# Reordered loads, stores and norm steps, and one scale for a batch's context, in a fused gated cross-attention and mixture-of-experts kernel

## The chip, the cores and the metric

The kernel runs on one core of a Trainium2 chip. The metric is device time of one execution in microseconds (us). Five engines work side by side, each through its own list of instructions in order: PE (TensorE, matrix multiplications and transposes; PEld is its loading of weights), ACT (ScalarE), DVE (VectorE), POOL (GpSimd) and SP (SyncE, which here only issues DMAs). They hold each other up by semaphores alone: an instruction waits until a counter has reached a value, and everything behind it on its engine waits too.

## The reference

`x` has 16 batches of 224 rows of 512; `ctx` has 16 batches of 750 rows of 512; there are 8 experts of hidden size 256.

```python
x = x + jnp.tanh(g_xattn[0]) * _L0_xattn_ref(_layernorm(x), ctx_1024, ctx_1024)
#   h = einsum('eth,efh->etf', x, ctx);  a = gelu(h);  einsum('etf,efh->eth', a, ctx)
x = x + jnp.tanh(g_ffn[0]) * _L0_ffn_ref(_layernorm(x), gate_w, w1, w2, w3)
#   softmax(x @ gate_w), the two best experts of each row, silu(xs @ w1) * (xs @ w3) @ w2
```

The softmax weight of an expert multiplies the row before it enters the expert. All is float32. The kernel computes a float32 product from float16 pieces: each operand is scaled by a power of two and split into a high and a low half, and three of the four products of halves are added.

## The kernel before

**Two phases.** The first takes the batches one by one in a software pipeline of 16 steps (`batches`, all written out, and `last_step`); step i finishes the attention of batch i, prepares batch i + 1 and loads batch i + 2. The second takes 63 blocks of 128 routed rows through the experts (`step2`, `blocks`). The change touches the first phase only.

**A step of the first phase on PE** (line 1277): the scores of batch i in three thirds of the context (`scores`, L1210), the attention output in three thirds (`attend`, L1222), and between them the transposes of the next context (`trans_ctx`, L1177), of the second norm's rows of batch i − 1 (`rows_norm2`, L1196 from `xf`) and of the first norm's rows of batch i + 1 (`rows_norm1`, L1196 from `xn`), the router's logits of batch i − 2, and one-column sums over partitions (`ctx_total` L1184, `weight_total` L1191).

**The scale of the context.** For each third q of a batch's context, ACT forms the sum of squares of each partition (`ctx_squares`, L594), whose elementwise result goes to a part of `ctx_part` that is free at that time. POOL makes powers of two from the sums (`all_rows_scale`, L439 to L444, writing `ctx_s` and its inverse, three columns). ACT writes the high half, third by third (`ctx_high_part`, L624), and DVE the low half (`context_low`, L825), after which SP may load the next batch over it. PE adds the sums of all partitions, ACT copies the total (`ctx_tot_out`, L610), and POOL makes the scale of the attention from the largest of three totals (`context_scale`, L459 and on), which DVE needs in `context_factors` (L817 to L819).

**What else stands in a step.** The 24 expert matrices are squared, scaled and split on the way: `weight_squares` L603, `weight_scale` L935 to L940, `weight_high` L658, `weight_low` L949. A matrix is taken by `own_matrix` in each step; an odd step begins a second one (`split_begin`) and the following even step ends it (`split_end`), so that an even step has two `weight_scale` and two `weight_low`, and an odd step one of each. The norm of batch i + 1 is `stats1` (DVE, L802, L805), `inv_std` (POOL, L432, L434, writing `rstd`) and `norm1` (DVE, L848). POOL then sends the routes of batch i − 3 by four indirect DMAs (`send_routes`, L489), raises e to the logits' differences of batch i − 2 (`exps`, L473), and only then makes the context's scale for batch i + 2. `a_low` (L834) splits the attention weights, `residual` (L863) makes x2, `xnT_low` (L855) splits the transposed norm, `route_top` (L882 to L900) finds the two best experts.

**Order.** Every engine's order is written out by hand in its `step`. SP's `step` (line 342) issues: the store of x2, the load of x, the loads of two thirds of the context, the store of the norm, the load of the last third, then one or two expert matrices. Each of these waits for what it needs, in that order.

Of the kernel before, what the change touches and what calls it, by code (L numbers as in the profile page):

```python
# [93 lines left out]
def build(nc, x, ctx, g_xattn, g_ffn, gate_w, w1, w2, w3, out):  # L94
# [4 lines left out]
    with st:  # L99
# [36 lines left out]
        ctx_part = [[sb(f"ctx_part{u}{h}", [CR, NC, D], F16) for h in range(2)] for u in range(2)]  # L136
# [161 lines left out]
        def _(sp):  # L298
# [43 lines left out]
            def step(i, u, h, load_two=True):  # L342
                if later(i, 1):
                    store_rows(i - 1)
                    load_x(i + 1, 1 - u)
                if load_two:
                    for q in range(NQ - 1):
                        sp.wait_ge(ctx_split, i * NQ + (NQ + q + 1))
                        load_ctx(i + 2, q)
                if later(i, 1):  # L350
                    store_norm(i - 1)
                if load_two:
                    sp.wait_ge(ctx_split, i * NQ + 2 * NQ)
                    load_ctx(i + 2, NQ - 1)
                for n in ((3 * h + 3,) if u else (3 * h + 1, 3 * h + 2)):
                    if n >= 2:
                        load_weight(*matrix(n))
# [46 lines left out]
        def _(pool):  # L404
# [31 lines left out]
            def scale_from(gmax, inv, s, bits=0, n=1):  # L436

                exp, exp_i = exp_f[:, 0, 0:n], exp_f[:, 1, 0:n].bitcast(I32)
                seq.done(g.tensor_scalar(exp_i, gmax.bitcast(I32), 0.5 ** (MANT + 1), None, ALU.mult))  # L439
                seq.hold()  # L440
                seq.done(g.tensor_scalar(exp, exp_i, float(ROOT), float(1 << MANT), ALU.add, ALU.mult))
                seq.hold()
                seq.done(g.tensor_scalar(inv, exp, float((TOP - 1 + bits) << MANT), None, ALU.subtract))
                return g.tensor_scalar(s, exp, -1.0, float((2 * BIAS + TOP - 1 + bits) << MANT), ALU.mult, ALU.add)  # L444
# [6 lines left out]
            def all_rows_scale(i, u):  # L451

                hold(pool, ctx_sum_ready, i * NQ + NQ)
                scale_from(ctx_sum[:, :], ctx_inv[u][:, :], ctx_s[u][:, :], 0, NQ).then_inc(ctx_scaled, NQ)

            def context_scale(i):

                hold(pool, ctx_gsum_ready, i + 1)
                seq.done(g.tensor_scalar(ctx_max[:, :], ctx_gsum[:, 0:1], ctx_gsum[:, 1:2], ctx_gsum[:, 2:3], ALU.max, ALU.max))  # L459
                seq.hold()  # L460
                scale_from(ctx_max[:, :], all_inv[:, :], all_s[:, :], A_BITS).then_inc(all_scaled, 1)
# [119 lines left out]
        def _(act):  # L581
# [14 lines left out]

            def weight_squares(n, kind, e):
# [21 lines left out]
            def ctx_high_part(i, u, q):  # L619
# [4 lines left out]
                a.activation(ctx_part[u][0][:, c, :], ctx_raw[0:CR, c, :], ACT.Copy, scale=ctx_s[u][0:CR, q:q + 1].bitcast(F32)).then_inc(ctx_high, 1)  # L624

# [56 lines left out]
            def step(i, u, h):  # L682
# [16 lines left out]
                else:  # L699
                    ctx_high_part(i + 1, w, 0)  # L700
                    ctx_high_part(i + 1, w, 1)
# [3 lines left out]
                ctx_high_part(i + 1, w, 2)  # L705
# [16 lines left out]
                if two:  # L722
                    ctx_squares(i + 2, 0)
                    ctx_squares(i + 2, 1)
                ctxT_out(i + 1, w, 4)
                if two:
                    ctx_squares(i + 2, 2)
# [60 lines left out]
        def _(dve):  # L788
# [175 lines left out]
            def step(i, u, h):  # L964
# [13 lines left out]
                if later(i, 1):  # L978
                    a_low(i, u, 1)
                    norm2(j)  # L980
                    context_factors(i + 1, w)
                split_end(weight_scale, i, u, h)
                stats1(i + 1, w, (h + u) * 16 + 16)
                context_low(i + 1, w, 1)
                split_end(weight_low, i, u, h)
                context_low(i + 1, w, 2)
                own_matrix(weight_scale, i, u, h)
                a_low(i, u, 2)
                if not later(i, 1):
                    context_factors(i + 1, w)  # L990
                norm1(i + 1, w)
                if later(i, 2):
                    route_top(i - 2)
                own_matrix(weight_low, i, u, h)
                xnT_low(i + 1, i * 4 + 2, w, 0, H_ps[w])
                xnT_low(i + 1, i * 4 + 3, w, 1)
            batches(dve, step)
# [448 lines left out]
```

## Time and profile before

| | us |
|---|---|
| median of 3 timed runs | 682.88 (682.84 to 685.06) |
| profiled execution, its own time | 682.06 |
| its span in the trace | 680.4 |
| first phase, first scores of batch 1 to the scores of batch 15 | 45.49 to 348.37 |
| even step / odd step (from rank to rank on PE, 196.21, 218.54, 239.46) | 22.33 / 20.92 |
| PE, ACT, DVE, POOL busy over the span | 632.9, 459.6, 416.5, 396.6 |

The steps repeat almost to the hundredth of a microsecond, so one even and one odd step stand for all from step 3 on. Step 8 (even) runs from 196.30 to 218.62 on PE, step 7 (odd) lies before it and step 9 (odd) behind it. A start time to the next start time on an engine is what an instruction costs its engine; the duration in a row is longer, since neighbours overlap by a tenth of a microsecond. The figure in square brackets is the idle time of the engine before the row, and what ended it.

### The profile page before, as it was taken

To read this page: it belongs to the slowest core of one execution; us is meant where nothing else is said; L and a number is where in the kernel's file an instruction comes from. 1 tells how busy PE (TensorE), PEld (TensorE's weight loads), DVE (VectorE), ACT (ScalarE), POOL (GpSimd) and SP (SyncE) were. 2 spreads that over 40 slices of the span, in tenths; PEclk is the share of its full clock that TensorE was granted. 3 is DMA by queue.
4 is the path that set the end of the run, shared out by engine and by line. 5 is a ranking of instruction groups with operands and counts; after the bars stand their busy time and mean duration, and the time that the engine had idled before them with its cause. 6 is when DMAs were issued, how large, how long until landed. Compare 5 with 4: busy or idle time off the path is not lost.

```text
span 680.4 us, 15835 instructions
## 1 busy us (share of the span) xinstructions
PE 632.9 (93%) x4638; PEld 443.5 (65%) x4639; DVE 416.5 (61%) x1287; ACT 459.6 (68%) x771; POOL 396.6 (58%) x460
## 2 busy tenths in 40 slices
PE   2789999999999999999998999999999999999990
PEld 1677788788887888878875555555555545555540
DVE  3468788988889888898896644553333333333330
ACT  5899999899999999999974344444434434434440
POOL 4332347765676556665567587776546555665561
PEclk9999999999999999999999999999999999999996
DMA  7455558656776658656424576566666667666663
GB/s 213 134 173 154 157 159 192 185 155 154 193 173 170 185 129 222 168 159 186 127 90 106 106 126 110 105 108 120 121 121 108 118 117 123 108 113 119 110 115 53
DMA packets 51604, 95.04 MB, mean 140 GB/s; under 512 B 17184, under 2 KB 25504, under 8 KB 51536
## 3 DMA queue, kind: packets, MB, share of 16 engines
q1 hardware_dynamic: 34240, 60.02, 33.2%
q0 software_dynamic: 16480, 34.15, 28.1%
q8 instruction: 36, 0.59, 0.4%
q14 instruction: 32, 0.26, 0.2%
q10 hardware_dynamic: 816, 0.02, 0.1%
HBM read 62.15 MB, written 32.01 MB: 138 GB/s over the span
## 4 chain that ended last, share of the span: by engine, by line
PE 39%; DMA 5%; DVE 3%; issue 2%; ACT 1%; POOL 1%; DVEq 0%; SPq 0%; POOLq 0%; ACTq 0%
PE bank L1368 21%; PE bank L1377 11%; DMA out_rows<-ctx_raw,meta 4%; PE bank L1323 4%; PE bank L1357 2%; DMA ctx_raw<-xf_rows,meta 1%; DMA meta<-route_table 0%; PE bank L1257 0%; PE bank L1222 0%; DVE ctx_part L825 0%; POOL out_rows L537 0%; DVEq L1145 0%; ACT ctx_part L624 0%; ACT ctx_raw L766 0%; DVE x L863 0%
## 5 line engine op out<-in xcount | busy, mean ns | idle before, releaser
L1368 PE MATMUL bank<-w,ctxT 128*128 x756 | 173.5, 379 | 0.6 <-issue 0.6
L537 POOL DMA_INDIRECT out_rows<-ctx_raw,meta x63 | 100.3, 1592 | 94.0 <-DMA out_rows<-ctx_raw,meta 77.5
L1222 PE MATMUL bank<-ctx_part,a_part 125*112 125x512 f16 x576 | 135.1, 380 | 0.8 <-DVE a_part L834 0.8
L1368 PEld LDWEIGHTS bank<-w,ctxT 128*128 128x128 f16 x756 | 73.9, 98 | 75.7 <-issue 0.7
L1210 PE MATMUL bank<-xnT,ctxT 128*125 128x224 f16 x1152 | 117.7, 261 | 0.3 <-ACT ctxT L629 0.3
L1210 PEld LDWEIGHTS bank<-xnT,ctxT 128*125 128x125 f16 x1152 | 111.9, 138 | 0.4 <-issue 0.4
L777 ACT ACTIVATE ctxT<-bank,cols 128x256 f32<-128x256 f32 x63 | 29.9, 474 | 115.0 <-issue 90.0
L1222 PEld LDWEIGHTS bank<-ctx_part,a_part 125*112 125x112 f16 x576 | 71.4, 130 | 39.6 <-DVE a_part L834 0.8
L629 ACT ACTIVATE ctxT<-bank 128x1000 f16<-128x1000 f16 x96 | 94.5, 1006 | 2.5 <-PE bank L1177 2.5
L1377 PE MATMUL bank<-w2s,ctxT 128*128 x378 | 91.9, 379 | 1.4 <-DVE ctxT L1137 1.3
L489 POOL DMA_INDIRECT route_table<-route,pos_i x64 | 72.7, 1136 | 18.2 <-issue 18.2
L525 POOL DMA_INDIRECT ctx_raw<-xf_rows,meta x67 | 67.3, 1005 | 21.0 <-issue 17.7
L1146 DVE TENSOR_SCALAR cols<-Q,meta 128x2 f32 x63 | 15.0, 238 | 104.4 <-ACT ctx_raw L766 64.3
L766 ACT ACTIVATE ctx_raw<-bank,cols 128x512 f32<-128x512 f32 x63 | 43.4, 688 | 52.2 <-PE bank L1377 52.2
L1155 DVE SCALAR_TENSOR_TENSOR ctxT<-bank,cols,ctxT 128x256 f32<-128x256 f32 x63 | 30.5, 484 | 62.8 <-issue 49.5
L1377 PEld LDWEIGHTS bank<-w2s,ctxT 128*128 128x128 f16 x378 | 36.9, 98 | 46.5 <-issue 4.8
L825 DVE SCALAR_TENSOR_TENSOR ctx_part<-ctx_raw,ctx_s,ctx_part 125x1024 f16<-125x1024 f32 x48 | 60.3, 1272 | 8.3 <-ACT ctx_part L624 8.3
L834 DVE SCALAR_TENSOR_TENSOR a_part<-a_f,factors,a_part 125x448 f16<-125x448 f32 x48 | 32.8, 683 | 37.1 <-ACT a_part L643 37.0
L1177 PE MATMUL bank<-ident,ctx_part 125*128 125x125 f16 x768 | 53.6, 220 | 1.6 <-ACT ctxT L629 1.1
L624 ACT ACTIVATE ctx_part<-ctx_raw,ctx_s 125x1024 f16<-125x1024 f32 x48 | 53.1, 1135 | 1.9 <-POOL ctx_s L444 1.9
L1177 PEld LDWEIGHTS bank<-ident,ctx_part 125*128 125x128 f16 x768 | 48.1, 99 | 8.2 <-issue 1.3
L594 ACT ACTIVATE ctx_part<-ctx_raw 125x1024 f16<-125x1024 f32 x48 | 50.3, 1048 | 1.1
(155 smaller groups left out, 986.8 us busy)
## 6 DMA issues: line engine op xcount, KB each, us to landing
ctx_raw<-in_ctx SPq DMA_DIRECT2D x48, 448.0 KB
w_raw<-in_L_ffn_w SPq DMA_DIRECT2D x24, 512.0 KB, 6.3
x<-in_x SPq DMA_DIRECT2D x16, 448.0 KB, 6.5
out_rows<-x SPq DMA_DIRECT2D x16, 448.0 KB
xf_rows<-xf SPq DMA_DIRECT2D x16, 448.0 KB, 4.6
ctx_raw<-in_ctx SPq DMA_DIRECT2D x48, 52.0 KB
meta<-route_table SPq DMA_DIRECT2D x67, 1.0 KB, 2.5
ctx_raw<-xf_rows,meta POOLq DMA_INDIRECT x67, 4.2
```

The lines of the kernel that those rows point to most:

```text
L489: g.indirect_dma_start(out=table, out_offset=bass.IndirectOffsetOnAxis(ap=pos_i[v][:, m:m + 1], axis=0), in_=route[v][:, t, k, :], in_offs ...
L525: g.indirect_dma_start(out=xg[n % AHEAD], out_offset=None, in_=src, in_offset=bass.IndirectOffsetOnAxis(ap=meta[n][:, 0:1], axis=0)).then_ ...
L537: g.indirect_dma_start(out=out, out_offset=bass.IndirectOffsetOnAxis(ap=meta[n][:, 0:1], axis=0), in_=y_sb[n % 2], in_offset=None, compute ...
L594: a.activation(ctx_part[i % 2][1][:, 2 * q:2 * q + 2, :], ctx_raw[0:CR, 2 * q:2 * q + 2, :], ACT.Square, accum_out=ctx_sum[0:CR, q:q + 1]) ...
L624: a.activation(ctx_part[u][0][:, c, :], ctx_raw[0:CR, c, :], ACT.Copy, scale=ctx_s[u][0:CR, q:q + 1].bitcast(F32)).then_inc(ctx_high, 1)
L629: a.activation(ctxT[u][:, :, c * CS:c * CS + CR], T_half[c % 2], ACT.Copy).then_inc(ctxT_ready, 1)
L825: v.scalar_tensor_tensor(ctx_part[u][1][:, c, :], ctx_raw[0:CR, c, :], ctx_s[u][0:CR, q:q + 1].bitcast(F32), ctx_part[u][0][:, c, :], ALU. ...
L1177: ins = t_.transpose(T_half[c % 2][:, h * KD + k, :], ctx_part[u][h][:, c, k * P:(k + 1) * P], ident16[0:CR, 0:CR])
L1210: ins = t_.matmul(dst, ctxT[u][:, hc * KD + k, c * CS:c * CS + CR], xnT[u][:, hx, k, :], start=j == 0, stop=j == KD * len(PARTS) - 1)
L1222: ins = t_.matmul(O_ps[t][0:TT, :], a_part[ha][:, c, t * TT:(t + 1) * TT], ctx_part[u][hc][:, c, :], start=c == 0 and (ha, hc) == PARTS[0] ...
L1368: ins = t_.matmul(H_ps[u][:, :], rows, w, start=m == 0, stop=m == KD * len(PARTS) - 1)
L1377: ins = t_.matmul(O_ps[u][:, :], rows, w2s[:, bass.ds(e * (KH * 2 * D) + (2 * k + part[1]) * D, D)], start=m == 0, stop=m == KH * len(PART ...
```

## The change

- SP: the load of x goes ahead of the store of x2 (with the wait on `x2_ready` that `store_rows` had), and all three thirds of the context are loaded ahead of the store of the norm.
- ACT: from batch 2 on one activation of 3072 columns squares the whole context (`row_squares`), in place of three of 1024; its elementwise result goes to half of both buffers of `ctx_part`, now one tensor. The high half of the last two thirds is one activation of 2048 columns (`ctx_high_rest`), which stands ahead of the total and of the second gelu.
- POOL: one scale per partition, written to all three columns by a broadcast; one total in place of the largest of three.
- DVE: in each step `split_end(weight_scale)` moves ahead of `norm2`; `norm1` ahead of `a_low(2)`; `split_end(weight_low)` from between the two `context_low` to behind `a_low(2)`; `own_matrix(weight_low)` behind both `xnT_low`.

```diff
@@ SP step
                 if later(i, 1):
+                    sp.wait_ge(x2_ready, i * 2)
+                    load_x(i + 1, 1 - u)
                     store_rows(i - 1)
-                    load_x(i + 1, 1 - u)
                 if load_two:
-                    for q in range(NQ - 1):
+                    for q in range(NQ):
                         sp.wait_ge(ctx_split, i * NQ + (NQ + q + 1))
                         load_ctx(i + 2, q)
                 if later(i, 1):
                     store_norm(i - 1)
-                if load_two:
-                    sp.wait_ge(ctx_split, i * NQ + 2 * NQ)
-                    load_ctx(i + 2, NQ - 1)
@@ POOL
-                scale_from(ctx_sum[:, :], ctx_inv[u][:, :], ctx_s[u][:, :], 0, NQ).then_inc(ctx_scaled, NQ)
+                scale_from(ctx_sum[:, 0:1], ctx_inv[u][:, :], ctx_s[u][:, :], 0, 1, NQ).then_inc(ctx_scaled, NQ)
...
+                gmax = ctx_gsum[:, 0:1]
+                if not later(i, 2):
+                    gmax = ctx_max[:, :]
+                    seq.done(g.tensor_scalar(gmax, ctx_gsum[:, 0:1], ctx_gsum[:, 1:2], ctx_gsum[:, 2:3], ALU.max, ALU.max))
@@ ACT
+            def row_squares(i, u):
+                for q in range(NQ):
+                    act.wait_ge(ctx_loaded[q], i * 32 + 32)
...
+                a.activation(ctx_both[u][:, :, 0:NC // 2, :], ctx_raw[0:CR, :, :].rearrange("p (h c) d -> p h c d", h=2), ACT.Square,
+                             accum_out=ctx_sum[0:CR, 0:1]).then_inc(ctx_sum_ready, NQ)
+            def ctx_high_rest(i, u):
+                act.wait_ge(ctx_scaled, i * NQ + NQ)
+                a.activation(ctx_part[u][0][:, 2:NC, :], ctx_raw[0:CR, 2:NC, :], ACT.Copy, scale=ctx_s[u][0:CR, 0:1].bitcast(F32)).then_inc(ctx_high, NQ - 1)
...
                     ctx_high_part(i + 1, w, 0)
-                    ctx_high_part(i + 1, w, 1)
+                    ctx_high_rest(i + 1, w)
                     ctx_tot_out(i + 1)
                     gelu(i, u, 1)
                 split_end(weight_tot_out, i, u, h)
-                ctx_high_part(i + 1, w, 2)
...
                 if two:
-                    ctx_squares(i + 2, 0)
-                    ctx_squares(i + 2, 1)
+                    row_squares(i + 2, u)
                 ctxT_out(i + 1, w, 4)
-                if two:
-                    ctx_squares(i + 2, 2)
                 ctxT_out(i + 1, w, 5)
@@ DVE step
                     a_low(i, u, 1)
+                split_end(weight_scale, i, u, h)
+                if later(i, 1):
                     norm2(j)
                     context_factors(i + 1, w)
-                split_end(weight_scale, i, u, h)
                 stats1(i + 1, w, (h + u) * 16 + 16)
                 context_low(i + 1, w, 1)
-                split_end(weight_low, i, u, h)
                 context_low(i + 1, w, 2)
                 own_matrix(weight_scale, i, u, h)
-                a_low(i, u, 2)
...
                 norm1(i + 1, w)
+                a_low(i, u, 2)
+                split_end(weight_low, i, u, h)
                 if later(i, 2):
                     route_top(i - 2)
-                own_matrix(weight_low, i, u, h)
                 xnT_low(i + 1, i * 4 + 2, w, 0, H_ps[w])
                 xnT_low(i + 1, i * 4 + 3, w, 1)
+                own_matrix(weight_low, i, u, h)
```

On DVE, in the middle of an even step, from the statistics of the next batch's rows (`stats`, `mv`) to the norm itself (`xn`), before:

```order
L802 BN_STATS stats<-x 112x6 x2
L805 BN_AGGR mv<-stats 112x2 x2
L825 SCALAR_TENSOR_TENSOR ctx_part<-ctx_raw,ctx_s,ctx_part 125x1024
L945 COPY w_inv<-w_scales 128x1
L949 SCALAR_TENSOR_TENSOR w<-w_raw,w_scales,w 128x4x256
L825 SCALAR_TENSOR_TENSOR ctx_part<-ctx_raw,ctx_s,ctx_part 125x1024
L935 TENSOR_SCALAR w_exp<-w_gsum 128x1
L937 TENSOR_SCALAR w_exp<-w_exp 128x1
L939 TENSOR_SCALAR w_scales<-w_exp 128x1
L940 TENSOR_SCALAR w_scales<-w_exp 128x1
L834 SCALAR_TENSOR_TENSOR a_part<-a_f,factors,a_part 125x448
L848 TENSOR_SCALAR xn<-x,mv,rstd 112x512 x2
```

The same place of the changed kernel, whose line numbers are higher by some 18 (L866 is the norm, L852 `a_low`, L967 `weight_low`):

```order
L820 BN_STATS stats<-x 112x6 x2
L823 BN_AGGR mv<-stats 112x2 x2
L843 SCALAR_TENSOR_TENSOR ctx_part<-ctx_raw,ctx_s,ctx_part 125x1024 x2
L953 TENSOR_SCALAR w_exp<-w_gsum 128x1
L955 TENSOR_SCALAR w_exp<-w_exp 128x1
L957 TENSOR_SCALAR w_scales<-w_exp 128x1
L958 TENSOR_SCALAR w_scales<-w_exp 128x1
L866 TENSOR_SCALAR xn<-x,mv,rstd 112x512 x2
L852 SCALAR_TENSOR_TENSOR a_part<-a_f,factors,a_part 125x448
L963 COPY w_inv<-w_scales 128x1
L967 SCALAR_TENSOR_TENSOR w<-w_raw,w_scales,w 128x4x256
```

A `weight_low` and an `a_low` that stood ahead of the norm stand behind it.

On DVE again, at the end of an even step, from the last instruction of `route_top` (`R`) to `residual` (`x`), before:

```order
L900 TENSOR_TENSOR R<-R,M 112x8
L945 COPY w_inv<-w_scales 128x1
L949 SCALAR_TENSOR_TENSOR w2s<-w_raw,w_scales,w2s 128x2x512
L855 SCALAR_TENSOR_TENSOR xnT<-bank,xnT 128x4x112 x2
L863 SCALAR_TENSOR_TENSOR x<-bank,factors,x 112x512 x2
```

The same place of the changed kernel:

```order
L918 TENSOR_TENSOR R<-R,M 112x8
L873 SCALAR_TENSOR_TENSOR xnT<-bank,xnT 128x4x112 x2
L963 COPY w_inv<-w_scales 128x1
L967 SCALAR_TENSOR_TENSOR w2s<-w_raw,w_scales,w2s 128x2x512
L881 SCALAR_TENSOR_TENSOR x<-bank,factors,x 112x512 x2
```

The step's own `weight_low` has changed places with the two `xnT_low`.

On ACT, from the squares at the end of an odd step (`ctx_sum` is the sum) to the middle of the next, even one, before:

```order
L594 ACTIVATE ctx_part,ctx_sum<-ctx_raw 125x1024 x2
L629 ACTIVATE ctxT<-bank 128x8x125
L594 ACTIVATE ctx_part,ctx_sum<-ctx_raw 125x1024
L629 ACTIVATE ctxT<-bank 128x8x125
L639 ACTIVATE a_f<-bank,factors 125x448
L643 ACTIVATE a_part<-a_f,factors 125x448
L624 ACTIVATE ctx_part<-ctx_raw,ctx_s 125x1024 x2
L610 ACTIVATE ctx_gsum<-bank 128x3
L639 ACTIVATE a_f<-bank,factors 125x448
L643 ACTIVATE a_part<-a_f,factors 125x448
L617 ACTIVATE w_gsum<-bank 128x1
L624 ACTIVATE ctx_part<-ctx_raw,ctx_s 125x1024
```

The same place of the changed kernel:

```order
L609 ACTIVATE ctx_part,ctx_sum<-ctx_raw 125x2x1536
L649 ACTIVATE ctxT<-bank 128x8x125 x2
L659 ACTIVATE a_f<-bank,factors 125x448
L663 ACTIVATE a_part<-a_f,factors 125x448
L639 ACTIVATE ctx_part<-ctx_raw,ctx_s 125x1024
L644 ACTIVATE ctx_part<-ctx_raw,ctx_s 125x2048
L625 ACTIVATE ctx_gsum<-bank 128x3
L659 ACTIVATE a_f<-bank,factors 125x448
L663 ACTIVATE a_part<-a_f,factors 125x448
L632 ACTIVATE w_gsum<-bank 128x1
```

The squares are one instruction, and 1024 more columns of the context's high half stand between the first gelu (the first `a_f`, `a_part`) and the second.

## Rows read from the trace of the kernel before

**Rows 1.** The page, busy time of each engine over the span:

```profile
PE 632.9 (93%) x4638; PEld 443.5 (65%) x4639; DVE 416.5 (61%) x1287; ACT 459.6 (68%) x771; POOL 396.6 (58%) x460
```

**Rows 2.** Windows of step 8 and step 9: length, then busy time per engine:

```profile
196.30:218.62 22.32, 21.46 (x200) 17.95 (x198) 19.11 (x61) 20.60 (x33) 13.99 (x19) 1.00 0.68 180
218.62:239.55 20.93, 20.93 (x199) 17.79 (x196) 18.04 (x57) 20.51 (x33) 13.64 (x19) 1.00 0.61 168
```

**Rows 3.** Timeline of PE and its weight loads, steps 0 and 8 (start, duration):

```profile
40.75 0.60 PE L1196 MATMUL bank<-ident,xn 112*128 112x112 f32 x4 [1.23 <-DVE xn L848]
...
211.89 0.39 PEld L1196 LDWEIGHTS bank<-ident,xf 112*128 112x128 f32 x4 [0.35 <-issue]
...
213.80 0.60 PE L1196 MATMUL bank<-ident,xn 112*128 112x112 f32 x4 [0.86 <-DVE xn L848]
```

**Rows 4.** Timeline of ACT, steps 7 and 8:

```profile
182.87 0.67 ACT L643 ACTIVATE a_part<-a_f,factors 125x448 f16<-125x448 f32 x1
183.44 1.13 ACT L624 ACTIVATE ctx_part<-ctx_raw,ctx_s 125x1024 f16<-125x1024 f32 x1
...
201.00 2.17 ACT L624 ACTIVATE ctx_part<-ctx_raw,ctx_s 125x1024 f16<-125x1024 f32 x2
...
217.00 1.05 ACT L594 ACTIVATE ctx_part<-ctx_raw 125x1024 f16<-125x1024 f32 x1
...
223.33 2.17 ACT L624 ACTIVATE ctx_part<-ctx_raw,ctx_s 125x1024 f16<-125x1024 f32 x2
```

**Rows 5.** Timeline of DVE, steps 7, 8 and 14:

```profile
183.57 0.69 DVE L834 SCALAR_TENSOR_TENSOR a_part<-a_f,factors,a_part 125x448 f16<-125x448 f32 x1 [0.27 <-ACT a_part L643]
...
187.07 2.45 DVE L825 SCALAR_TENSOR_TENSOR ctx_part<-ctx_raw,ctx_s,ctx_part 125x1024 f16<-125x1024 f32 x2
...
204.49 0.69 DVE L834 SCALAR_TENSOR_TENSOR a_part<-a_f,factors,a_part 125x448 f16<-125x448 f32 x1 [0.27 <-ACT a_part L643]
...
208.49 1.25 DVE L825 SCALAR_TENSOR_TENSOR ctx_part<-ctx_raw,ctx_s,ctx_part 125x1024 f16<-125x1024 f32 x1
...
209.72 1.27 DVE L949 SCALAR_TENSOR_TENSOR w<-w_raw,w_scales,w 128x1024 f16<-128x1024 f32 x1
...
213.20 1.00 DVE L848 TENSOR_SCALAR xn<-x,mv,rstd 112x512 f32<-112x512 f32 x2
...
215.92 1.27 DVE L949 SCALAR_TENSOR_TENSOR w2s<-w_raw,w_scales,w2s 128x1024 f16<-128x1024 f32 x1
217.11 1.14 DVE L855 SCALAR_TENSOR_TENSOR xnT<-bank,xnT 128x448 f16<-128x448 f32 x2
...
334.23 0.69 DVE L834 SCALAR_TENSOR_TENSOR a_part<-a_f,factors,a_part 125x448 f16<-125x448 f32 x1 [0.27 <-ACT a_part L643]
...
347.98 1.40 DVE L863 SCALAR_TENSOR_TENSOR x<-bank,factors,x 112x512 f32<-112x512 f32 x2
```

**Rows 6.** Timeline of POOL, steps 7 and 8:

```profile
195.45 2.96 POOL L473 TENSOR_TENSOR ex<-euler,dl 112x16 f32<-112x16 f32 x1
199.14 0.26 POOL L439 TENSOR_SCALAR exp_f<-ctx_sum 128x3 int32<-128x3 int32 x1 [0.73 <-ACT ctx_part L594]
...
209.98 1.61 POOL L434 TENSOR_TENSOR rstd<-ve,neg_half 112x2 f32<-112x2 f32 x1
...
216.11 1.89 POOL L489 DMA_INDIRECT route_table<-route,pos_i  x1 [0.30 <-issue]
218.02 2.97 POOL L473 TENSOR_TENSOR ex<-euler,dl 112x16 f32<-112x16 f32 x1
221.46 0.26 POOL L439 TENSOR_SCALAR exp_f<-ctx_sum 128x3 int32<-128x3 int32 x1 [0.48 <-ACT ctx_part L594]
...
222.55 0.19 POOL L444 TENSOR_SCALAR ctx_s<-exp_f 128x3 int32<-128x3 f32 x1
...
223.19 0.73 POOL L434 TENSOR_TENSOR rstd<-ve,neg_half 112x2 f32<-112x2 f32 x1
```

**Rows 7.** Transfers into the raw context (the second phase's gathers among them), issue to landing:

```profile
DMA to landing us min/median/max: 3.3/4.8/6.2
```

## What was predicted

> **What bounds the kernel now.** I read the page first: PE is busy for 93% of the span, no other engine for more than 68% [rows 1]. The second phase isn't touched, so the question is what limits a step of the first. The windows of one even and one odd step answer half of it: in the odd step PE is busy for all of its 20.93 us, in the even step for 21.46 of 22.32 [rows 2]. The timeline of PE shows the hole in the even step: 0.86 of waiting for `xn`, DVE's norm, and just before it 0.35 in its weight loads [rows 3]. Without both an even step would take PE 21.1, an even and an odd step (a pair) 42.05 in place of 43.25.
>
> Who else needs most of a pair? ACT is busy for 20.5 us of each step [rows 2], but what matters is a ring that passes through ACT, DVE and POOL once per step. I follow it from where ACT begins the high half of the context (201.00) to where it does so a step later (223.33) [rows 4]. Two thirds and the second gelu: DVE starts `a_low(1)` at 204.49, so 3.49. DVE's chain to the end of the statistics, where `context_low(1)` starts: 208.49, so 4.00. POOL's `inv_std` and four route DMAs up to `exps` at 218.02: 9.53. `exps` 2.97. Then POOL waits 0.48 for ACT's squares, of which I count 0.1 as the hold itself, and makes the scale from 221.46 to 222.74: 1.28. ACT takes it up 0.59 later, 0.05 more than none [rows 4 to 6]. Without the two spare pieces (0.38 and 0.54) the ring needs 21.4 of the even step's 22.33. In the odd step, the same way: 3.49 again, then 183.57 to 187.07 is 3.50, to 195.45 is 8.38, 2.96, 0.1, 1.28, 0.05: 19.75 of 20.92, spare 1.17. So the ring of a pair needs 41.2: the slack under PE's own 42.05 is 0.9 us, and this kernel has a second limit right below the first.
>
> **The change part by part.**
>
> *Norm sooner.* In the even step DVE ends the second `context_low` 1.26 sooner, since a `weight_low` (209.72, 1.27 long) leaves, and the `a_low` of 0.6 ahead of the norm leaves too. The norm at 213.20 could start 1.8 sooner; but it needs POOL's `rstd`, which ends at 211.59 (209.98 + 1.61) [rows 5, 6], and there it stays: the gain is 1.6 against 0.86 + 0.35 of waiting, so PE's hole goes. What is late next is `a_low(2)`, which now follows the norm: the third `attend` needs it some 1.65 after the norm starts, when PE is 0.8 beyond its first `xn` transposes; that is a tie within 0.1.
>
> *One activation of 3072 for the squares.* ACT's 1.05 for 1024 columns [rows 4] and its slope, (1.13 − 0.67) over 576 columns, 0.80 ns each [rows 4], make 2.7 for the whole against three times 1.05: 0.45 less. It is hidden in both kinds of step, where ACT then waits for PE or for POOL. Bounds of the long one: 2.5 to 3.1.
>
> *One activation of 2048 for the rest of the high half.* It costs ACT 1.0 + 0.82 in place of 1.0 + 1.0, and no one waits for the last third earlier than it comes now. But 1024 columns of it now stand ahead of the second gelu, on the ring. That is +0.82 (0.80 to 1.04 by the rows used) on 3.49, in every step. The ring becomes 22.25 + 20.55 = 42.8: above PE's 42.05. So the second limit takes over.
>
> *One total, one scale.* One POOL instruction fewer before `context_factors`; DVE gets there later than POOL anyhow: nothing. The squares end sooner, so POOL's waits of 0.48 and 0.73 for them go; they were the spare pieces counted above.
>
> *Loads ahead of stores.* x comes some 0.4 sooner, the last third of the context without the norm's 448 KB ahead. Neither is waited for in the trace of before, so nothing gained; the stores behind them are wanted a step later. The matrices are loaded later, since `weight_low` moves to the step's end; the load that waits for it on SP stands ahead of the next load of x, but that one waits for `residual`, which is behind `weight_low` on DVE: nothing more is held. The matrix is squared in the next step only, behind both its first gelus: nothing, or some tenths.
>
> *`weight_low` behind `xnT_low`.* This is what I think costs. POOL's instructions are held when they start inside a long DVE one: `rstd`'s power takes 1.61 when it starts in `weight_low` and 0.73 when nothing runs, and the route DMA at 216.11 takes 1.89, ending as the `weight_low` of 215.92 has ended [rows 5, 6]. In the changed even step, counted from the norm's start n: norm and `route_top` 2.72 (213.20 to 215.92), `a_low(2)` 0.6, `weight_low` 1.25, two `xnT_low` 1.07; so the last `weight_low` runs from n + 5.6 to n + 6.85. POOL: a first route DMA to n + 1.5 (held by the norm as now), a second that now starts in the first `weight_low` and ends at n + 3.65, then two free ones of 0.95 with gaps of 0.3: `exps` starts at n + 6.2, in the middle of `weight_low`, and is held for 0.65. The route DMAs lose less than now (about 0.2 less), and `rstd` 0.05. In the odd step, where the first `weight_low` is missing and `xnT_low` waits for ACT, the same durations put `weight_low` at n + 4.85 to n + 6.05 and `exps` at n + 5.3: held 0.7. So even 22.25 + 0.65 − 0.25 = 22.65, odd 20.55 + 0.7 = 21.25: a pair takes 43.9, 0.65 more than before. Of this hold no row shows `exps` itself: it takes 2.96 or 2.97 in both steps [rows 6]. The bounds are no hold (42.55 a pair, −0.7) and a hold of `exps` and then of the scale's last instruction by the next `a_low(0)`, 0.4 a step (44.65, +1.4). I take 43.9, since the nearest row, a POOL power that starts in a `weight_low`, was held to its end.
>
> The Trainium skill, SBUF — State Buffer, section "Who interferes with whom", says that a VectorE instruction with two SBUF inputs contends with a GpSimd instruction that reads SBUF, and one with at most one SBUF input does not. The held rows agree. By that page `exps` would be held (43.9 a pair); by its own rows, which show 2.97 at most, 42.55.
>
> *The ends.* Step 0: PE waits 1.23 for `xn` [rows 3]; the norm now goes ahead of `a_low(2)`, and 1.1 comes back. Steps 1 and 2 have no routes for POOL to send, so their ring is short: step 1 gets ACT's savings, some 0.3, step 2 its hole of 1.2 less 0.2 for the tie. Together −2.4 (−1 to −3). After step 14, DVE's residual opens the block map from which the second phase's loads are made. It is 13.75 behind `a_low(1)` now (334.23 to 347.98), with no idle time between [rows 5]; the same instructions remain, `a_low(1)` is 0.85 later in the ring and the norm waits 0.2 for `rstd`: +1.05.
>
> **The sum.** Five pairs (steps 4 to 13): 5 × 0.65 = +3.25; −2.4 + 3.25 + 1.05 = +1.9. The profiled execution took 682.06, which makes 684.0; the median of the runs before is 682.88, 0.8 above it, so I forecast 684.8. With the bounds of a pair alone: −4.85 to +5.65, so 678 to 688.5.
>
> **The rivals.**
>
> *PE stays the only limit.* POOL's second route DMA starts only 0.2 us behind the beginning of `weight_low`; if it gets in ahead of it, the chain behind it is 0.75 shorter, `exps` comes before the last `weight_low`, and the ring is 42.05 or less. For it: margins of 0.2 are what I can't place; the odd step's POOL chain has room today. Against: the long activation on the ring is certain. The time: 5 × −1.2, −2.4 and at the end +0.6: −7.8, 675.1.
>
> *The ring binds, but `exps` is not held*, as its own rows have it: −0.7 a pair, 678.
>
> *Slower: ACT waits for the context.* The one squaring needs all three thirds; before, the last third was wanted 3 us later than the first. The squares begin 3.8 behind the norm now (213.20 to 217.00) and would begin 4.0 behind it [rows 4, 5]; the last third is issued some 0.7 ahead of the norm, so it has 4.7 to land. The median of the tile's transfers is 4.8 and the longest 6.2 [rows 7]. At the longest ACT is 1.5 late in each step, and from there it is ACT's path, not POOL's, that sets the ring: 22.2 + 22.7 = 44.9 a pair, 5 × 1.65 − 2.4 + 1.05 = +6.9, 689.8. It decides as soon as a landing takes over 4.7 + 0.6. Against: one 448 KB store fewer ahead of it.
>
> **How the numbers follow.** The forecast's mechanism gets 0.52 (its own range 681 to 688.5), PE alone 0.22, the ring without the hold 0.12, the late context 0.10; 0.04 is left for what I don't see. A measurement of this kernel tells about 0.5%, 3.4 us, from no change: below 679.5 is faster, above 686.3 slower. Faster: PE alone 0.22, of the third 0.07: 0.29. Slower: 0.09 of the late context and 0.16 of the forecast, whose upper end has `a_low(0)` holding the scale: 0.25. The same: 0.46. The range reaches from 675, which leaves half of the PE case out, to 689.5.
>
> **What would show it.** POOL's first scale instruction behind `exps` has no wait for ACT any more; ACT's first third waits for POOL's `ctx_s` in each step; `exps` takes 3.5 or more where it took 2.97; PE waits for `xn` in the odd steps too, some 0.5 to 1; a pair from rank to rank is near 43.9. I am wrong if PE has no waits (PE alone), if `exps` is 2.97 everywhere, or if ACT's squaring waits for a DMA.

## The result and the profile after

Six runs of the changed kernel took 691.76 us in the median (690.44 to 692.23), six of the kernel before beside them 682.86 (681.14 to 687.06). The ratio is 1.0118, 95% interval 1.0096 to 1.014: slower by 1.2%, and 2 us beyond the range that was given. The profiled execution took 691.75 us, its span is 690.0 us.

The page's busy line answers to [rows 1]: ACT and POOL do less than before (450.7 for 459.6, 381.0 for 396.6), PE more (641.5 for 632.9) with the same count of PE's instructions.

```profile
PE 641.5 (93%) x4638; PEld 446.1 (65%) x4639; DVE 418.4 (61%) x1287; ACT 450.7 (65%) x701; POOL 381.0 (55%) x446
```

The windows of steps 8 and 9, from rank to rank, answer to [rows 2] (length, busy time of PE, PEld, DVE, ACT and POOL, granted clock, share of the DMA engines, GB/s). The even step lost 0.25, the odd one 0.93, and PE is now short of its window in both (0.82 and 0.35 idle). The loss is in part longer busy time: of the odd step's 0.93 the idle time is 0.35.

```profile
198.62:221.19 22.57, 21.75 (x199) 18.00 (x197) 18.72 (x59) 20.12 (x28) 13.21 (x18) 1.00 0.68 167
221.19:243.05 21.86, 21.51 (x197) 17.85 (x195) 18.77 (x58) 20.16 (x28) 12.52 (x18) 1.00 0.76 171
```

By PE's rank products the whole account is short. At the start of step 3 the changed kernel is 0.79 us ahead, at the start of step 15 it is 5.74 behind (354.02 against 348.28), at the first product of the second phase 8.59 (377.15 against 368.56), at the end of the span 9.6. So the twelve steps 3 to 14 lose 6.5 us (pair 44.37 in place of 43.28), and step 15 and what follows 3.

ACT's waits, summed over the run (us, times, longest), hold two lines that before did not exist:

```profile
ACT ctx_part L609 <- DMA ctx_raw<-in_ctx: 10.9, 10, 1.9
ACT ctx_part L609 <- PE bank L1241: 2.1, 3, 0.7
```

The second is the same wait: there, too, ACT starts 0.22 to 0.23 behind the landing of the last third (by the semaphore records of the trace), and the `attend` that is named had been done before. So ACT waited for the load ahead of 13 of its 14 squarings of a whole context, 13.1 us in all. One turn shows where this sits. ACT's timeline of step 8 (answers to [rows 4]; L609 is the one squaring, L644 the 2048 columns, L659 a gelu):

```profile
204.10 1.13 ACT L639 ACTIVATE ctx_part<-ctx_raw,ctx_s 125x1024 f16<-125x1024 f32 x1
205.15 1.99 ACT L644 ACTIVATE ctx_part<-ctx_raw,ctx_s 125x2048 f16<-125x2048 f32 x1
...
207.09 0.62 ACT L659 ACTIVATE a_f<-bank,factors 125x448 f32<-125x448 f32 x1
...
220.74 2.76 ACT L609 ACTIVATE ctx_part<-ctx_raw 125x3072 f16<-125x3072 f32 x1 [0.96 <-DMA ctx_raw<-in_ctx]
```

DVE's in the same step (answers to [rows 5]): the second `a_low`, the last two low parts, the norm, and at the end the own matrix's `weight_low` ahead of the residual.

```profile
208.44 0.68 DVE L852 SCALAR_TENSOR_TENSOR a_part<-a_f,factors,a_part 125x448 f16<-125x448 f32 x1 [1.14 <-ACT a_part L663]
...
212.50 2.45 DVE L843 SCALAR_TENSOR_TENSOR ctx_part<-ctx_raw,ctx_s,ctx_part 125x1024 f16<-125x1024 f32 x2
...
215.63 1.01 DVE L866 TENSOR_SCALAR xn<-x,mv,rstd 112x512 f32<-112x512 f32 x2 [0.18 <-issue]
...
221.28 1.28 DVE L967 SCALAR_TENSOR_TENSOR w2s<-w_raw,w_scales,w2s 128x1024 f16<-128x1024 f32 x1
222.48 1.40 DVE L881 SCALAR_TENSOR_TENSOR x<-bank,factors,x 112x512 f32<-112x512 f32 x2
```

SP's queue issues the last third 0.03 after DVE has let its room go, and the norm's store 0.80 behind it:

```profile
214.98 0.76 SPq L308 DMA_DIRECT2D ctx_raw<-in_ctx  x2
...
215.78 0.34 SPq L340 DMA_DIRECT2D xf_rows<-xf  x1
```

The low parts end at 214.95. The third lands at 220.52 by its semaphore record, 5.54 behind its issue, and ACT, which was ready at 219.78, starts at 220.74. That is a ring: first third of the high part (204.10) to `a_low` 4.34, to the end of the low parts 6.51, from there through the load to ACT's start 5.79, squaring to the next first third (226.52) 5.78, together 22.42, where PE alone would need 21.1. In the steps in which ACT waited, the way from the end of the low parts to ACT's start took 5.4 to 6.7 us, of which the third's own time from issue to landing was 5.2 to 6.5 (median 5.5).

[rows 7] has no such load in it. Before, as after, the profile lists the loads of the context without a landing time (the first line, of the kernel before); the 4.8 is made of the second phase's gathers into the same tile and of writes of output rows that read it:

```profile
ctx_raw<-in_ctx SPq DMA_DIRECT2D x48, 448.0 KB
ctx_raw<-xf_rows,meta POOLq DMA_INDIRECT x67, 4.2
out_rows<-ctx_raw,meta POOLq DMA_INDIRECT x63, 4.9
```

By the semaphore records of the trace before, the last third took 5.4 to 6.5 us from issue to landing in steps 3 to 14 as well. In step 8 it was issued at 212.22, landed at 217.58, and its squaring began at 220.17, so there were 2.4 us to spare; over these steps 1.6 to 2.4.

POOL's `exps` (answers to [rows 6]) are held in the odd steps and free in the even ones, and the first scale instruction still waits for ACT in the even ones:

```profile
198.01 3.97 POOL L477 TENSOR_TENSOR ex<-euler,dl 112x16 f32<-112x16 f32 x1
...
220.57 2.97 POOL L477 TENSOR_TENSOR ex<-euler,dl 112x16 f32<-112x16 f32 x1
...
223.76 0.25 POOL L438 TENSOR_SCALAR exp_f<-ctx_sum 128x1 int32<-128x1 int32 x1 [0.23 <-ACT ctx_part L609]
```

PE still waits for the norm, 0.33 to 0.71 in nearly every step, the odd ones too (answers to [rows 3]); the last row is step 15's:

```profile
216.24 0.60 PE L1215 MATMUL bank<-ident,xn 112*128 112x112 f32 x4 [0.71 <-DVE xn L866]
...
238.10 0.60 PE L1215 MATMUL bank<-ident,xn 112*128 112x112 f32 x4 [0.35 <-DVE xn L866]
...
362.02 4.16 PE L1241 MATMUL bank<-ctx_part,a_part 125*112 125x512 f16 x12 [1.25 <-DVE a_part L852]
```

### The profile page after: what moved, and what is told of

It is laid out like the page before. It is cut to its first block, busy times and chain, and to the rows that moved or that the text cites. A ratio compares the mean times of both kernels' runs of the same rounds, so it can differ in the third digit from the quotient of the medians.

```text
span 690.0 us, 15723 instructions
## 1 busy us (share of the span) xinstructions
PE 641.5 (93%) x4638; PEld 446.1 (65%) x4639; DVE 418.4 (61%) x1287; ACT 450.7 (65%) x701; POOL 381.0 (55%) x446
## 4 chain that ended last, share of the span: by engine, by line
PE 38%; ACT 15%; DVE 14%; DMA 13%; issue 12%; POOL 6%; DVEq 1%; SPq 0%; ACTq 0%; POOLq 0%
PE bank L1387 19%; PE bank L1396 10%; DMA ctx_raw<-in_ctx 7%; DMA out_rows<-ctx_raw,meta 5%; ACT ctx_part L644 4%; DVE ctx_part L843 3%; PE bank L1342 3%; ACT ctxT L649 3%; DVE stats L820 2%; ACT a_f L659 2%; PE bank L1241 2%; DVE xf L895 2%; PE bank L1376 2%; ACT ctx_part L639 2%; ACT a_part L663 1%
## 5 line engine op out<-in xcount | busy, mean ns | idle before, releaser
L1241 PE MATMUL bank<-ctx_part,a_part 125*112 125x512 f16 x576 | 137.1, 384 | 2.0 <-DVE a_part L852 1.9
L1241 PEld LDWEIGHTS bank<-ctx_part,a_part 125*112 125x112 f16 x576 | 71.7, 130 | 44.1 <-DVE a_part L852 4.8
L649 ACT ACTIVATE ctxT<-bank 128x1000 f16<-128x1000 f16 x96 | 92.8, 1003 | 3.1 <-PE bank L1196 3.1
L493 POOL DMA_INDIRECT route_table<-route,pos_i x64 | 62.2, 972 | 19.8 <-issue 14.2
L431 POOL TENSOR_SCALAR ve<-mv 112x2 f32<-112x2 f32 x32 | 19.9, 623 | 70.2 <-DVE mv L823 69.5
L852 DVE SCALAR_TENSOR_TENSOR a_part<-a_f,factors,a_part 125x448 f16<-125x448 f32 x48 | 32.7, 681 | 38.3 <-ACT a_part L663 36.1
L477 POOL TENSOR_TENSOR ex<-euler,dl 112x16 f32<-112x16 f32 x14 | 47.3, 3378 | 4.7 <-DVE dl L909 4.5
```

The costliest lines, as they stand in the source:

```text
L477: ins = g.tensor_tensor(ex[:, :, :].rearrange("p t e -> p (t e)"), euler[:, :], dl[:, :, :].rearrange("p t e -> p (t e)"), ALU.pow)
L493: g.indirect_dma_start(out=table, out_offset=bass.IndirectOffsetOnAxis(ap=pos_i[v][:, m:m + 1], axis=0), in_=route[v][:, t, k, :], in_offs ...
L649: a.activation(ctxT[u][:, :, c * CS:c * CS + CR], T_half[c % 2], ACT.Copy).then_inc(ctxT_ready, 1)
L1241: ins = t_.matmul(O_ps[t][0:TT, :], a_part[ha][:, c, t * TT:(t + 1) * TT], ctx_part[u][hc][:, c, :], start=c == 0 and (ha, hc) == PARTS[0] ...
```

## The experiments

Theory A: the ring just shown, closed by ACT's one squaring that waits for the last third. Theory B: the forecast's ring over POOL with `exps` held. C: SP's order of transfers. D: the place of the own `weight_low` in DVE's order. Each kernel was timed in five rounds; ratios are to the kernel before, with their 95% intervals.

**Parts alone (e1, e2, e3) and the squaring's wait taken away (e4b).**

e1, the DVE part of the change alone:

```
+ split_end(weight_scale, i, u, h)    # ahead of norm2
  norm1(i + 1, w)
+ a_low(i, u, 2)
+ split_end(weight_low, i, u, h)
  ...
  xnT_low(i + 1, i * 4 + 3, w, 1)
+ own_matrix(weight_low, i, u, h)
```

> The kernel before with VectorE's new order alone (norm1 ahead of the third a_low and of the split matrix's weight_low, the own matrix's weight_low last); squares, scales and SyncE's order as before. Theory A (the loss of the changed kernel is ScalarE's one squaring waiting for the context's last third, so the loop runs through that load): the last squaring here needs only 0.95 us behind its third, so the loop has no such ring; the steps take 43.2 to 43.4 us a pair as before, the end gains or loses up to 3 us (the residual of batch 14 stands behind one more weight_low): 682 to 686. Theory B (the forecast's ring over POOL, with the exponentials held by the moved weight_low): the exponentials take 3.9 us instead of 2.96 in odd steps, and the pair grows by 0.65: 685 to 688.

686.39 us, 1.0051 [1.0035, 1.0066]. The profiled execution has a pair of 44.1, but unevenly: steps of 21.1 and steps of 23 to 24.6. In the long ones ACT waits up to 1.27 us for the last third (4.0 in all), or PE up to 1.79 us for the norm. The longest of them shows why, in DVE's timeline: the statistics wait for x, which SP issued at 221.78 behind a matrix (220.07) and a store.

```profile
232.38 1.29 DVE L802 BATCH_NORM_STATS2 stats<-x 112x6 f32<-112x512 f32 x2 [2.57 <-DMA x<-in_x]
```

So DVE's order alone costs, in the steps too, which A had not expected. The time lies inside B's range (685 to 688) and just outside A's, but not by B's mechanism: `exps` are held (3.97 or 3.98) in only three of the twelve steps, and ACT waits for POOL's scale `ctx_s` twice in the whole run. The granted clock also falls to 0.50 twice (at 205 to 207 and at 239 to 241), which is a part of the loss. The place of the own `weight_low` (D) fits the wait for x just shown; e1 moves other instructions too, so it doesn't show D by itself.

e2, SP's part alone:

```
+ sp.wait_ge(x2_ready, i * 2); load_x(i + 1, 1 - u)
  store_rows(i - 1)
+ for q in range(NQ): ... load_ctx(i + 2, q)    # all three
  store_norm(i - 1)
```

> The kernel before with SyncE's new order alone (x ahead of the store of the rows, the context's last third ahead of the store of the norm). Theory A: the last third is issued 0.1 to 1 us earlier and shares the DMA engines with the norm's store, its landing stays 4.8 to 5.8 us; ScalarE's last part of squares (0.95 us) has room: 682 to 684, pair 43.2. Theory B: no part of POOL's ring changes: 682 to 684. A theory C, that the order of the transfers itself costs the time: 686 or more here.

682.62 us, 0.9997 [0.9985, 1.0008], pair 43.28: nothing. C falls.

e3, ACT's and POOL's part alone, the orders of DVE and SP as before:

```
- def step(i, u, h):  # VectorE, SyncE: new order
+ def step(i, u, h):  # VectorE, SyncE: order of before
```

> The changed kernel with VectorE's and SyncE's order of before, so only one squaring, one scale, and thirds 1 and 2 of the high parts in one instruction. Theory A: the squaring still waits for the last third (issued after the norm's store): ScalarE waits for DMA ahead of it in most steps, pair 44 or more, 687 to 692. Theory B: exponentials are not held (2.96 in odd steps too), POOL does fewer scales, the pair falls to 42.8: 679 to 683.

707.0 us, 1.0373 [1.0351, 1.0396], pair 46.1: nearly three times the change's loss. ACT waits 10.9 us for the last third, and PE again 0.86 for the norm in most steps. B, which wanted a gain, falls here. The size is beyond A's 692. Part of the rest is in ACT's waits for DVE's `weight_scale`, 24.9 us in the run for 13.2 before: in DVE's order of before it stands behind `norm2`, and the 2048 columns delay the gelu ahead of that (argued from the orders, not tested by itself). In most even steps they take 1.57 and 1.02; ACT's copy `xfT` stands behind them, and PE waits 1.3 to 1.8 for it in six (11.3 us in the run for `xfT`). One step of 27.57 ran partly at a lower granted clock (0.88 over the step).

e4b, the change with a squaring that reads the first third three times:

```
- for q in range(NQ): act.wait_ge(ctx_loaded[q], i * 32 + 32)
+ act.wait_ge(ctx_loaded[0], i * 32 + 32)
- ctx_raw[0:CR, :, :].rearrange(...)
+ ctx_raw[0:CR, 0:1, :].rearrange(...).to_broadcast([CR, 2, NC // 2, D])
```

> The changed kernel, whose squaring reads the first third three times over instead of the three thirds once, so it has the same size and place but waits for the first third alone; the waits for the other two stand ahead of the high parts in the next step. The scale is that of a third of the context here. Theory A: ScalarE no longer waits for DMA ahead of the squaring, the pair falls by about 1.1 from 44.4 to 43.3 or below; what is left against before is the end (about +3): 683 to 686. Theory B: the ring over POOL stands unchanged, exponentials 3.97 in odd steps: 690 to 692.

682.56 us, 1.0003 [0.9985, 1.0021]: the 8.9 us by which the change was behind the kernel before are gone with that wait alone, a little more than A had (683 to 686). B's 690 to 692 falls. (`exps` take 2.96 in most of its steps, with DVE's order unchanged, so that order alone doesn't fix the hold.) Its squarings never wait and still take 2770 ns. Undisturbed pairs take 42.36; two of the six take 44, where ACT waited 0.99 and 0.55 for a matrix that came late. The windows of one good and one bad pair (length, PE):

```profile
173.19:194.22 21.03, 21.03 (x198) 17.86 (x196) 18.57 (x58) 20.06 (x28) 13.52 (x18) 1.00 0.71 177
194.22:215.55 21.33, 21.33 (x200) 18.05 (x197) 18.71 (x59) 19.83 (x28) 12.42 (x18) 1.00 0.73 172
215.55:237.39 21.84, 21.45 (x198) 17.94 (x195) 18.64 (x58) 19.80 (x28) 13.28 (x18) 1.00 0.76 175
237.39:259.65 22.26, 21.56 (x200) 18.02 (x197) 18.72 (x59) 19.96 (x28) 13.60 (x18) 1.00 0.64 165
```

**The ring shortened (e5), the own `weight_low` moved back (e6, e7), and three squarings (e8).**

```
e5  - ctx_high_rest(i + 1, w)            # 2048 columns ahead of the gelu
    + ctx_high_part(i + 1, w, 1)
      ctx_tot_out(i + 1); gelu(i, u, 1); split_end(weight_tot_out, i, u, h)
    + ctx_high_part(i + 1, w, 2)
e6  + own_matrix(weight_low, i, u, h)    # ahead of the two xnT_low again
      xnT_low(...); xnT_low(...)
    - own_matrix(weight_low, i, u, h)
e7  both;   e8  before, with SP's new order and DVE's as in e6
```

> The changed kernel with thirds 1 and 2 of the high parts in two instructions again, third 2 behind the split matrix's total as before; one squaring and one scale stay. Theory A with the ring squaring, scale, high parts, second gelu, a_low, VectorE's last two low parts, load of the last third, next squaring: this ring is shorter by 0.85 us a step (the second gelu no longer stands behind 2048 columns), the waits for DMA ahead of the squaring (10.9 us in ten) mostly go, pair 43.0 to 43.5, 683 to 687. Theory D (what costs is only where VectorE splits the own matrix, not the ring): 690 to 692.

> The changed kernel with the own matrix's weight_low ahead of the two xnT_low again. Theory A: the ring over the last third stays as it is and so do most of the waits for it, pair 44.0 to 44.4; the end gains about 2 to 3 us, since the residual of batch 14 and the first map come sooner: 687 to 690. Theory D (SyncE's next weight load and x stand behind that weight_low in its queue, and that delays the rest): x lands sooner, the exponentials take 2.96 in odd steps, TensorE no longer waits for xn, pair 43.0 to 43.4: 682 to 685.

> Both edits at once: own weight_low ahead of xnT_low, and the high parts of thirds 1 and 2 in two instructions. Theory A: the ring has a slack of half a us, pair 42.4 to 43.0, the end as before: 676 to 681. Theory D: what e6 gives, and no more: 682 to 685.

> The kernel before (three squarings, three scales, high parts in three) with SyncE's new order and VectorE's norm1 ahead of the third a_low and of the split matrix's weight_low, but the own matrix's weight_low left ahead of xnT_low. Theory A: only the last third's own squaring (1.05 us) follows its load, no wait for it; xn comes 2 us sooner and the 0.7 to 1.3 us a pair that TensorE waited for it go: pair 42.1 to 42.6, 675 to 680. Theory D: the same, since the own weight_low is where it was. Theory B (ring over POOL with its three scales): 43.3, 682 to 684.

e5: 679.23 us, 0.995 [0.9931, 0.997], pair 42.56; e6: 689.46, 1.0105 [1.0081, 1.0128], pair 44.55; e7: 679.81, 0.9964 [0.9948, 0.998], pair 42.98; e8: 681.51, 0.9987 [0.9978, 0.9997], pair 43.34. Against the kernel before, timed beside each, the change is 8.9 us behind and e5 2.8 ahead: 0.85 us of ACT's work, taken off the ring and put behind the gelu, gives back 11.7 us, near the 14 × 0.85 = 11.9 of a ring that sets every step. That is more than A had for e5 (683 to 687), and D's 690 to 692 falls. ACT still waits for the third, 10.2 us ahead of 13 squarings (6.1 of it under that name in the profile), but what is left of these waits is mostly no longer PE's. The 0.85 are taken off the ring over POOL as well, so e5 alone doesn't tell A from B; e4b does, and ACT's waits for `ctx_s`, two of 1.8 us together in the changed kernel, both in the first steps. With the own `weight_low` ahead of `xnT_low` PE gets the last half of the norm late, up to 1.2 us in every second step, as e8 shows at the start of its scores:

```profile
219.56 0.69 PE L1209 MATMUL bank<-xnT,ctxT 128*125 128x224 f16 x5 [1.08 <-DVE xnT L853]
```

So the ring of A stands, and D is wrong about the steps: its 682 to 685 for e6 falls, and norm sooner pays only with that `weight_low` last (e8 against the pair of e12 below). A's ranges hold for e6 and e7 (e6's pair is a little longer than the 44.0 to 44.4 expected). For e8 A's 675 to 680 was too low: PE waits 7.7 us there for `xnT`, in seven places. e8's time and pair are those that B gave, but ACT waits for `ctx_s` only twice there, so its mechanism is not seen.

**The end (e10), the norm's store (e11), and the orders without the one squaring (e12, e13).**

```
e10  e5, and  + if i == B - 2: own_matrix(weight_low, i, u, h)   # step 14, ahead of xnT_low
              - own_matrix(weight_low, ...)                      # last, in the other steps
e11  e10, and SP:  load_weight(...)
                 + store_norm(i - 1)
e12  before, with DVE's order of e10 and SP's new order
e13  before, with DVE's and SP's orders as in the change
```

> The run with the high parts split again (e5), with the own matrix's weight_low ahead of the two xnT_low in step 14 alone, so that VectorE begins batch 14's residual 1.4 us sooner there, and last as before it in all other steps. Theory A: steps as in e5 (pair 42.6); in step 15 the first a_low is through before TensorE wants it, TensorE doesn't wait 1.26 us and its attends go at 220 ns again, not 390: 2 to 3 us off 679.2, so 676 to 677.5. Theory D (the end's loss is SyncE's or the meta loads', not the residual's place): 678.5 to 680.

> As e10, with SyncE's store of the norm behind the weight loads, so that the context's last third has the DMA engines without it. Theory A: the last third lands in 4.8 us or less instead of 5.5 to 5.8, the 6.1 us that ScalarE still waits for it in e5 go, pair 42.2 to 42.4: 674 to 676. A rival: the store comes so late that VectorE's next norm2 or SyncE's next x load waits, and the pair rises to 43 or more: 679 or more.

> The kernel before (three squarings, three scales, high parts in three) with VectorE's new order (step 14 as in e10) and SyncE's new order. Theory A: its last squaring is only a third of the work behind the last load, so there is no wait for it; the pair is 42.2 to 43, and the time 675 to 679: one squaring and one scale bring nothing of their own. A rival: POOL's two more scales and ScalarE's two more instruction starts a step keep the pair at 43.3: 681 to 684.

> The kernel before with VectorE's and SyncE's new orders just as in the changed kernel, and ScalarE's and GpSimd's part as before (three squarings, three scales): the complement of e3. Theory A (the one squaring and the 2048 columns ahead of the second gelu are the whole loss in the steps, the place of the own weight_low in step 14 the loss at the end): pair 42.1 to 42.3 as in e12, and 2 to 3 us at the end more than it, 676 to 678. Theory D (VectorE's order with the own matrix last costs in the steps too, as when it was tried alone): 683 to 687.

e10: 677.81 us, 0.9943 [0.9923, 0.9963], just above A's 677.5; its interval overlaps that of e5. In the profiled executions the stretch from step 15's rank to the second phase is 21.55 for 23.0 in e5, and no wait of 1.25 is left; the end is worth 1.4 us by that. e11: 679.59, 0.9959 [0.9937, 0.9981]: no gain over e10, and A's 674 to 676 fails. From issue to landing the third took 4.6 to 5.7 us (median 5.15; in e10 5.0 to 5.6, median 5.3), so the store beside it is a small part of its landing, and the expected 4.8 is missed. ACT's waits for it fall from 7.1 us ahead of 13 squarings to 4.8 ahead of nine. But the profiled execution (674.89) is e11's fastest, and the runs reach 688.77; what the slower ones lost, perhaps by the rival's late store, this trace doesn't show.

e12: 674.39 us, 0.9888 [0.9869, 0.9908], the fastest of all; e13: 676.10, 0.9898 [0.9879, 0.9917], in A's range, while D's 683 to 687 falls. (e13's profiled execution, 681.72, is slower than its median, with three steps in which a matrix or x came late; its steps are not used.) The windows of two steps of e12:

```profile
191.10:212.24 21.14, 21.14 (x199) 18.00 (x197) 18.84 (x61) 20.49 (x33) 12.25 (x19) 1.00 0.65 178
212.24:233.16 20.92, 20.92 (x198) 17.78 (x195) 18.70 (x58) 20.50 (x33) 13.62 (x19) 1.00 0.75 178
```

PE is busy for all of the 42.06, with ACT doing its three squarings, three high parts and 20.5 us a step as before. The four corners, in us (ratio):

| | orders of before | new orders of DVE and SP |
|---|---|---|
| three squarings, three scales | 682.4 (1) | 676.1 (0.990) |
| one squaring, one scale, 2048 columns | 707.0 (1.037) | 691.8 (1.012) |

One half of the change gains 1%, the other loses 2% or more with either order. The gain needs both orders: SP's alone gave 0.9997, DVE's alone 1.0051, the two together 0.990. That fits the long step of e1, where x stood in SP's queue behind a store that SP's new order puts behind x; no run shows it by itself. With e10's orders the one squaring still costs something without the 2048 columns ahead of the gelu: a pair of 42.56 in e10, 42.11 in e12.

## Why the prediction was wrong

*PE alone needs 42.05 a pair.* Right: e12 takes 42.06 in the two steps shown and 42.11 over six pairs, and 674.39 beside the 675.1 that this rival gave, though for another kernel than the one forecast.

*Which ring binds.* This step failed: the forecast put ACT's wait for the last third of the load at nothing. The 0.82 us of `ctx_high_rest` were sized well (1.99 against 1.13 is 0.86), but I laid them on the ring over POOL alone. They lie also on the ring over the load, which starts with the same gelu and `a_low`, leaves by DVE's last low part and SP, and comes back through the squaring. Before, that ring had slack, 1.6 to 2.4 us a step, for only a third of the squares stood behind the last load. The one squaring put all 2.76 us there, 1.7 more than 1.05, and the 2048 columns 0.86: 2.6 together, more than the slack. "No one waits for the last third earlier than it comes now" was the wrong sentence; I priced the high parts by who reads them and not by whose room they free. In its place the runs show ACT waiting for that load ahead of 13 of 14 squarings, 13.1 us; the loss of 8.9 us gone when the squaring doesn't wait (e4b); and 11.7 us back for 0.85 a step taken off this ring (e5).

*The late context as a rival.* Its mechanism was the right one and its places were right: the third is issued 0.65 ahead of the norm (0.7 said), and ACT is ready 4.15 behind it (4.0 said). The term that was mis-sized is the landing: the 4.8 of [rows 7] holds no load of the context, and by the semaphore records such a third took 5.4 to 6.5 us from issue to landing already before the change, 5.2 to 6.5 in it, against the 4.7 that I gave it and the 5.3 from which I had it decide. What I set against it, one store fewer ahead, failed too: the store came 0.8 behind and went at the same time. It had a tenth of the chance. Its 689.8 is near the 691.76 partly by luck: its pair of 44.9 is longer than the 44.37 measured, and its ends, −1.35 together, were −0.8 and +2.9.

*The hold of `exps`.* Half right. It takes 3.97 in odd steps (3.5 or more said), 2.97 in even ones, where its start now lies ahead of the own `weight_low`, because the route DMAs take 0.95 to 1.07 and were not held as I had counted (the second starts 0.12 ahead of the first `weight_low`, where I had it 0.2 behind). My reading of the route DMA of 216.11 was wrong: it ends at 218.00, not as the `weight_low` beside it ends, at 217.19. The Trainium skill, SBUF — State Buffer, section "Who interferes with whom", has a VectorE instruction with two SBUF inputs contend with a GpSimd instruction that reads SBUF; the 3.97 beside `weight_low` and the 2.97 ahead of it agree. As a limit it doesn't count: in step 8 POOL's scale still waits for ACT's squares, and of the signs that I gave, ACT's first third waiting for `ctx_s` in each step did not come: it waits twice in the run. In e12 `exps` takes 2.96 or 2.97 in all but one of the steps from 105.94 to 316.38 (3.97 at 274.69), with the same order in DVE; in step 8 it starts at 211.51, 0.7 ahead of the own `weight_low` (212.22), which then takes its usual 1.27.

*Norm sooner.* The waits of PE, 0.86 and 0.35, were to go. They stay at 0.35 to 0.71 in the changed kernel, since ACT's lateness moves all of DVE's low parts and the statistics behind them; without the ring (e12) they go. PE's wait in the odd steps was one of my signs of `exps` held; it came for this other reason.

*The ends.* The early steps gave 0.8 of the 2.4; the squarings of steps 1 and 2 already waited 0.93 and 0.98 for the third. The end cost 2.9 up to the second phase where I had +1.05. I had counted the residual's delay and not what follows it: the block map of DVE stands ahead of step 15's first `a_low`, so PE waits 1.25 us, and after that wait its clock is lower (below).

*Weights.* I wrote that nothing more is held when `weight_low` goes last. SP's next matrix waits for that very instruction, and x is queued behind it: in e1 and e4b ACT and PE then wait behind either, now and then, up to 1.8 us (DVE up to 2.57). e12's profiled execution has none of these waits.

## What to carry to other kernels

Before merging instructions that each follow a part of a load into one that needs the whole, write down the ring that runs through the load (who frees the room, issue, landing, first use) with the landing of that very load, not a median under the tile's name that other transfers make up; a saving of starts on an engine with slack is worth nothing against a microsecond there. A change of several parts is worth splitting by engine: here one half gained 1% and the other lost more, and of the gaining half neither part gained alone. After moving work to the end of a step, look at what the last step has behind it.

## What was not expected of the hardware

TensorE's granted clock fell to half, 1.2 GHz, behind a short wait. In step 15 of the changed kernel PE runs sixteen products of 8 columns and two of one, waits 1.25 us, and begins the `attend`; the windows (length, PE, PEld, DVE, ACT, POOL, clock) show full clock up to 363, then a fall to half, and full again from 367:

```profile
360.00:362.00 2.00, 0.77 (x8) 0.68 (x7) 1.86 (x9) 1.03 (x3) 0.00 (x0) 1.00 0.73 286
362.00:363.00 1.00, 0.98 (x5) 0.64 (x6) 1.00 (x2) 0.73 (x2) 0.00 (x0) 1.00 0.03 12
363.00:364.00 1.00, 1.00 (x5) 0.57 (x4) 0.83 (x8) 0.00 (x0) 0.23 (x1) 0.65 0.13 17
364.00:365.00 1.00, 1.00 (x4) 0.49 (x3) 0.58 (x1) 0.92 (x1) 0.94 (x1) 0.50 0.07 1
...
366.00:367.00 1.00, 1.00 (x9) 1.00 (x8) 0.56 (x3) 0.17 (x1) 0.68 (x2) 0.64 0.05 1
367.00:368.00 1.00, 1.00 (x13) 1.00 (x12) 0.99 (x5) 0.68 (x1) 0.72 (x1) 1.00 0.78 95
```

The twelve products of the `attend` behind that wait take 4.16 us there and 2.8 in e12 and e10, where PE does not wait at that place; in e12 the clock stays at 1.00. So the wait and the slower products behind it cost 2.6 us. In e5, where the wait is 1.26, the same twelve take 4.33. In e12 a wait of 1.13 us at the start of the same step, behind sixteen products of 125 columns and two of 16, left the clock at 1.00. The length of the wait is not all of it: in e1 the twelve take 4.48 us at 203.30, at a clock of 0.50, behind sixteen products of 8 columns, two of one and a wait of only 0.26, and 2.80 at 180.81, at full clock, behind sixteen products of 8 columns and a wait of 0.17. What decides between them no run here shows.
